# The first stage of a convolution and feed-forward kernel: other queue orders, integers cast by their transfers, x1 evicted in pairs, normalisation on POOL

## The reference

```
xn   = layernorm(x)                         # over the 256 features
# branch 1
z    = layernorm(xn) * gamma + beta
proj = z @ W_in + b_in                      # 768 columns: v, x1, x2 of 256 each
y    = causal_conv(v,  k0) * x1             # along the 4096 tokens, per channel
y    = causal_conv(y,  k1) * x2
a    = xn + y @ W_out + b_out
# branch 2
h    = silu(xn @ (w_gate/127).T) * (xn @ (w_up/127).T)
f    = h @ (w_down/127).T
out  = x + a + f
```

## Time and profile before

| what | value |
|---|---|
| median of three runs | 362.04 us |
| the profiled execution: its own time, its span | 361.94 us, 360.2 us |
| PE busy | 310.2 us, 86% |
| DVE busy | 250.2 us, 69% |
| POOL busy | 196.3 us, 54% |
| ACT busy | 182.8 us, 51% |
| mean granted TensorE clock | 0.957 |
| DMA | 81.00 MB, 225 GB/s on the mean |
| first matmul of the first convolution | 98.46 us from the span's start |

### The profile page before, as it was taken

The page is one execution under the profiler, slowest core; times in us unless marked ns, Lnnn a source line. Parts: engine busy times, 40 slices in busy tenths (PEclk is TensorE's granted clock), DMA queues, the critical chain, the costliest instruction groups (busy, mean ns, idle before and its releaser), DMA issues.

```text
span 360.2 us, 11764 instructions
## 1 busy us (share of the span) xinstructions
PE 310.2 (86%) x4940; PEld 243.2 (68%) x4940; DVE 250.2 (69%) x523; ACT 182.8 (51%) x383; POOL 196.3 (54%) x268
## 2 busy tenths in 40 slices
PE   0737573988398999999999999999999999998995
PEld 0425452777385777777777777877777776657994
DVE  1794996678436566666766668857766766787995
ACT  1464444799134444434444444444444444449993
POOL 3699077357746667567667675686676663210000
PEclk9976958799989999999999999999999999999999
DMA  7995300006068696786886887957868879500445
GB/s 252 341 340 163 131 1 2 4 12 224 2 235 322 226 387 243 278 349 237 322 326 249 352 291 262 379 226 300 348 230 332 323 251 378 206 0 3 140 154 177
DMA packets 22072, 81.00 MB, mean 225 GB/s; under 512 B 2050, under 2 KB 13186, under 8 KB 13826
## 3 DMA queue, kind: packets, MB, share of 16 engines
q1 hardware_dynamic: 21026, 79.04, 59.2%
q10 hardware_dynamic: 992, 1.18, 1.0%
HBM read 75.50 MB, written 4.72 MB: 223 GB/s over the span
## 4 chain that ended last, share of the span: by engine, by line
PE 55%; DVE 15%; ACT 11%; POOL 8%; issue 6%; DMA 3%; POOLq 0%; DVEq 0%; SPq 0%; ACTq 0%
PE bank_c L271 14%; PE bank_p L271 11%; PE bank_u L271 10%; PE bank_g L271 10%; PE bank_d L271 9%; ACT vx L695 3%; DMA res<-in_L_attn_x 3%; ACT vx L687 3%; DVE stats L726 2%; ACT xr L586 2%; DVE hhl L869 2%; DVE x1y L747 1%; DVE sgh L864 1%; DVE pmw L850 1%; ACT ybuf L575 1%
## 5 line engine op out<-in xcount | busy, mean ns | idle before, releaser
L271 PE MATMUL bank_d<-wd,hhl 128*128 128x256 f16 x384 | 84.3, 271 | 0.3 <-DVE hhl L869 0.2
L271 PEld LDWEIGHTS bank_p<-wq,xT 128*128 128x128 f16 x1536 | 71.5, 99 | 16.8 <-issue 1.7
L271 PE MATMUL bank_p<-wq,xT 128*128 128x64 f16 x1536 | 80.9, 194 | 2.1 <-issue 2.1
L271 PE MATMUL bank_u<-xT,wgu 128*128 128x512 f16 x192 | 66.2, 378 | 0.4 <-DVE sgh L864 0.4
L271 PE MATMUL bank_g<-xT,wgu 128*128 128x512 f16 x192 | 66.2, 377 | 0.0
L271 PEld LDWEIGHTS bank_c<-vhl,bands 128*128 128x128 f16 x1024 | 50.0, 97 | 22.5 <-issue 7.2
L271 PE MATMUL bank_c<-vhl,bands 128*128 128x64 f16 (+3 forms) x1024 | 58.3, 186 | 6.5 <-POOL vhl L1073 5.5
L271 PEld LDWEIGHTS bank_c<-ybuf,bands 128*128 128x128 f16 x1024 | 51.7, 96 | 17.9 <-issue 1.2
L1067 POOL TENSOR_TENSOR vx<-vx,bias 128x512 f32<-128x512 f32 x32 | 39.2, 1226 | 42.7 <-DVE vx L755 42.7
L271 PE MATMUL bank_c<-ybuf,bands 128*128 128x64 f16 (+3 forms) x1024 | 60.3, 184 | 0.8 <-DVE ybuf L889 0.8
L625 ACT CAST hhl<-sgh 128x512 f16<-128x512 f32 x48 | 29.7, 619 | 41.6 <-DVE sgh L864 41.6
(11 more groups left out here) (168 smaller groups left out, 539.7 us busy)
## 6 DMA issues: line engine op xcount, KB each, us to landing
bands<-taps_seq SPq DMA_DIRECT2D x64, 1024.0 KB, 8.1
out<-res SPq DMA_DIRECT2D x8, 512.0 KB, 2.9
res<-in_L_attn_x SPq DMA_DIRECT2D x3, 1024.0 KB, 10.4
res<-in_L_attn_x SPq DMA_DIRECT2D x2, 512.0 KB, 8.5
bands<-in_L_attn_W_in ACTq DMA_DIRECT2D x1, 768.0 KB, 5.9
bands<-in_L_ffn_w_gate SPq DMA_DIRECT2D x1, 768.0 KB, 10.0
bands<-in_L_ffn_w_up SPq DMA_DIRECT2D x1, 768.0 KB, 10.2
vx<-in_L_ffn_w_down SPq DMA_DIRECT2D x1, 768.0 KB, 10.1
```

The lines of the kernel that those rows point to most:

```text
L271: return nc.tensor.matmul(o, w, m, start=start, stop=stop, skip_group_check=True)
```

## The change

- SP's queue loads x blocks 0 to 3, then W_in, x 4 to 7, x 8 to 15, the taps, x 16 to 23, x 24 to 31, b_out, W_out. ACT's queue loads gamma and beta as two rows of 128 each (PE transposes them, a new step at the front of its program) and b_in. CUTS becomes 0, 4, 8, 16, 24, 32.
- POOL's queue loads the three integer tensors into float32 tiles, so the transfers cast them. `pair` on POOL is gone: PE transposes the unscaled values (`transpose_pair`), ACT rounds with the scale, DVE splits with the scale.
- ACT normalises blocks 0 to 7, POOL 8 to 31 (NA = 8).
- `project` trails the transposes by LV = 5 blocks, `project_x1` by LX = 8. x1 is evicted two blocks at a time and without its bias: pairs 0 to 9 by ACT (JA = 10), two instructions each, 10 to 15 by DVE, one instruction each. POOL adds the x1 bias a group of channels at a time, in the main stage one group ahead.
- The integer pairs come one a block from block 28 (PAIR0); the program branches after block 22 (FORK).
- DVE's statistics come one or two blocks at a time, its maxima at b = 10, 12 and 14, and the constants in four parts. POOL's taps and scales are spread over its loop.
- One residual ahead of the groups, not four; three in groups 1 to 3 and two in groups 4 to 14.

```diff
-    CUTS = (0, 4, 12, 20, 28, NB)
+    CUTS = (0, 4, 8, 16, 24, NB)
+    LV = 5
+    LX = 8
+    NA = 8
+    JA = 10
+    PAIR0 = 28
+    FORK = 22
...
+            load_x(0)
+            sp.dma_start(win[:, :, :], W_in.rearrange("(k p) n -> p k n", p=P)).then_inc(win_loaded, 16)
+            load_x(1)
+            load_x(2)
...
+            load_x(3)
+            load_x(4)
...
-                            sp.wait_ge(unit_ready, HB)
+                            sp.wait_ge(unit_tp, HB)
...
+            pe.wait_ge(gb_loaded, 32)
+            nc.tensor.transpose(w_bank[:, 0:2 * KD], gb_row[:, :], ident32[0:2 * KD, 0:2 * KD]).then_inc(gb_tp, 1)
...
-                pe.wait_ge(unit_ready, q + 1)
                 if q > 0:
                     pe.wait_ge(unit_l, q)
+                src, _ = pair_src(q)
...
+                if 0 <= b - LX < NB:
+                    project_x1(b - LX)
+                if 0 <= b - PAIR0 < PAIRS:
+                    transpose_pair(b - PAIR0)
...
+            def evict_x1(j):                                     # ACT
+                act.wait_ge(x1_mm, 2 * j + 2)
+                for b in (2 * j, 2 * j + 1):
...
+                    last = nc.scalar.activation(x1y2[:, :, b:b + 1].rearrange("p c o -> p (c o)"), o, ACT.Copy, scale=col(r2r, b))
+                last.then_inc(x1a_ready, 1)
...
+            def evict_x1(j):                                     # DVE
+                dve.wait_ge(x1_mm, 2 * j + 2)
...
+                nc.vector.tensor_tensor(x1y2[:, :, pair], bank_c[j % 2][:, :].rearrange("p (b c) -> p c b", b=2), scales,
+                                        ALU.mult).then_inc(x1v_ready, 1)
...
+            for b in range(1, NB + LX + 5):                      # DVE
+                if b <= 4:
+                    layernorm_stats(2 * b + 6, 2 * b + 8)
+                elif b <= 16:
+                    layernorm_stats(b + 11, b + 12)
+                elif b <= 18:
+                    layernorm_stats(2 * b - 6, 2 * b - 4)
                 if b - 1 < NB:
                     split_x(b - 1)
...
+                if b in (10, 12, 14):
+                    if b == 10:
+                        dve.wait_ge(int_loaded, 48)
...
+            def normalise(b):                                    # POOL
+                if b == NA or b in CUTS:
+                    pool.wait_ge(r_ready, batch_of(b) + 1)
+                pool.wait_ge(x_tp, b - 3)
+                nc.gpsimd.tensor_scalar(xn[:, b % 4, :], res[:, b, :], col(r1, b), col(nmr, b), ALU.mult, ALU.add).then_inc(xnp_ready, 1)
...
+            first_scales(0)
+            second_scales(0)
+            first_scales(1)
+
+            pool.dma_start(gu_f[:, 0:HB, :], w_gate.rearrange("(u p) d -> p u d", p=P)).then_inc(int_loaded, 16)
+            pool.dma_start(gu_f[:, HB:2 * HB, :], w_up.rearrange("(u p) d -> p u d", p=P)).then_inc(int_loaded, 16)
+            pool.dma_start(wd_f[:, :, :], w_down.rearrange("(a p) h -> p a h", p=P)).then_inc(int_loaded, 16)
+            second_scales(1)
+            for b in range(4, NB + LX):
+                if b == 4:
+                    first_scales(2)
+                if b == 5:
+                    second_scales(2)
+                if NA <= b + 2 < NB:
+                    normalise(b + 2)
+                if b == 7:
+                    pool.wait_ge(bin_ready, 1)
+                    nc.gpsimd.tensor_tensor(bias[:, :], bin_row, scl, ALU.mult).then_inc(bias_ready, 1)
+                if b in (8, 9):
+                    scale_taps(b - 8)
...
+                if b == 13:
+                    first_scales(3)
+                if b == 15:
+                    second_scales(3)
+                if b == 21:
+                    first_scales(4)
+                if b == 23:
+                    second_scales(4)
+                if b in (16, 24, 32, 38):
+                    add_bias((16, 24, 32, 38).index(b))
+                if b in (22, 30, 37):
+                    split_v((22, 30, 37).index(b))
+            split_v(3)
+            add_x1_bias(0)
...
             for G in range(NG):                                  # POOL
+                for b in residuals_of(G):
+                    residual(b)
                 gate_1(G, 0)
                 gate_1(G, 1)
+                if G < NG - 1:
+                    add_x1_bias(G + 1)
```

More of the change, by code:

```diff
@@ L479, in body @@
             def body(general):
-                for b in range(FORK, NB + 4):
+                for b in range(FORK, NB + LX):
                     first_stage(b)
@@ L554, in _ @@
             for dst, src, s in (
-                (win[:, :, :], W_in.rearrange("(k p) n -> p k n", p=P), win_loaded),
-                *((gb[:, i, k:k + 1], a[k * P:(k + 1) * P].rearrange("(p o) -> p o", o=1), gb_loaded)
-                  for i, a in enumerate((gamma, beta)) for k in range(KD)),
+                *((gb_row[i * KD:(i + 1) * KD, :], a.rearrange("(k p) -> k p", p=P), gb_loaded) for i, a in enumerate((gamma, beta))),
                 (bin_row[:, :], bass.AP(b_in.tensor, b_in.offset, [[0, P], [1, 3 * D]]), bin_loaded),
@@ L574, in normalise @@
                     act.wait_ge(x_tp, b - 3)
-                nc.scalar.activation(xn[:, b % 4, :], res[:, b, :], ACT.Identity, bias=col(nmr, b), scale=col(r1, b)).then_inc(xn_ready, 1)
+                nc.scalar.activation(xn[:, b % 4, :], res[:, b, :], ACT.Identity, bias=col(nmr, b), scale=col(r1, b)).then_inc(xna_ready, 1)
             def round_x(b):
@@ L1092, in taps, with split_taps, add_x1_bias @@
                 link(last)
-                for v, (taps, where) in enumerate(spans):
-                    nc.gpsimd.tensor_tensor(kpd[:, :, v, 1, where], taps, kpd[:, :, v, 0, where], ALU.subtract).then_inc(kpad_ready, 1)
+            def split_taps(v):
+                taps, where = spans[v]
+                nc.gpsimd.tensor_tensor(kpd[:, :, v, 1, where], taps, kpd[:, :, v, 0, where], ALU.subtract).then_inc(kpad_ready, 1)
+            def add_x1_bias(G):
+                if G == 0:
+                    pool.wait_ge(x1a_ready, JA)
+                    pool.wait_ge(x1v_ready, NB // 2 - JA)
+                tile = x1y2[:, G * CG:(G + 1) * CG, :]
+                row = bias[:, :]
+                off = bass.AP(row.tensor, row.offset + D + G * CG, [row.ap[0], [1, CG], [0, NB]])
+                nc.gpsimd.tensor_tensor(tile, tile, off, ALU.add).then_inc(x1_biased, 1)
@@ L1103, in _ @@
-            layernorm_scales(1)
-            taps()
-            layernorm_scales(2)
-            pool.wait_ge(bin_ready, 1)
-            nc.gpsimd.tensor_tensor(bias[:, :], bin_row, scl, ALU.mult).then_inc(bias_ready, 1)
-            layernorm_scales(3)
-            add_bias(0)
-            layernorm_scales(4)
-            pool.wait_ge(ffn_consts, 1)
-            for q in range(PAIRS):
-                if q == 3 or q == 7:
-                    add_bias((q + 1) // 4)
-                pair(q)
-                if q in (1, 5):
-                    split_v(q // 4)
@@ L1119, in _, with residuals_of @@
+            split_v(3)
+            add_x1_bias(0)
             pool.wait_ge(bout_loaded, 16)
             residual(0)
-            residual(1)
-            add_bias(3)
-            residual(2)
-            residual(3)
-            split_v(3)
+            def residuals_of(G):
+                first, n = (3 * G - 2, 3) if G < 4 else (2 * G + 2, 2)
+                return range(first, first + n) if 0 < G < NG - 1 else ()
             def gate_1(G, h):
```

276 lines of the change are left out of this document (150 added, 126 removed).

## The result

Four runs of the changed kernel took 350.55 to 354.43 us, median **352.55**. The kernel before took 362.05 beside them (360.8 to 362.51). The ratio is 0.9723, 95% interval 0.9686 to 0.976: faster by 2.8%. Forecast were 348.7 and a range of 343 to 358, so the time lies inside, 3.9 us above the forecast.

The account below looks back on a forecast made before the run. The middle was taken as bound by PE's own work, the first stage by several bounds in turn. S 13.6 us earlier and 0.4 more behind it give -13.2: 361.9 becomes 348.7 us, range 343 to 358.

Parts of the forecast that it names:

- S: Start of the first convolution, the one moment the change moves: 98.46 us before, forecast at 84.9.
- Step 1: Startup up to the scaled weights: ready at 14.8 us, against 20.17 before; the 5.4 us head start not all kept.
- Step 2: POOL until block 8: three transfers hold it 6.3 us at no cost; it normalises block 8 from 28.0 us.
- Step 3: Blocks 8 to 27: POOL becomes slowest; PE reaches the branch at about 52 us, gap 3.7, block 28 at 64.
- Step 4: Integer pairs, one a block from block 28, each waiting for the last: 2.03 us apiece, pair 8 starting at 81.4.
- Step 5: Behind S: POOL's x1 bias additions fall in its idle time; 0.4 us more, in group 0.
- A: First stage: integers land late, holding up DVE and then PE; 366 us, chance 0.08.
- B: Main stage: POOL's extra work surfaces, 0.37 to 0.6 us in each of 15 groups; 356 us, chance 0.13.
- C: First stage: POOL is a quarter slower than its quiet durations, 8 us on 34; 355 us, chance 0.14.
- D: First stage: branch gap partly hidden or ACT's eviction cheap, 3 to 5 us less; 344.5 us, chance 0.08.
- E: First stage hardly moves, the new order being held back elsewhere; time within 0.5%, chance 0.03.

Follow-up runs that it names:

- experiment 2: Changed kernel with the old queue order for W_in, gamma and beta, without PE's transpose of gamma and beta: 355.95 us.
- experiment 11: Changed kernel with ACT normalising all blocks again, and DVE's statistics in bursts with the three maxima together: 357.14 us.
- experiment 10: Changed kernel with all sixteen pairs of x1 blocks evicted by DVE, none by ACT (JA = 0): 352.79 us.
- experiment 5: Changed kernel with the integer pairs in two PSUM banks in turn, starting at block 31 instead of 28: 345.92 us.
- experiment 3: Changed kernel with an integer pair every second block from block 22 instead of one a block from 28: 345.5 us.
- experiment 12: Changed kernel with two pair banks from block 31, ACT normalising 12 blocks, residuals 0 to 5 in the first stage, last round_v ahead of last round_pair: 340.56 us.
- experiment 7: Changed kernel with POOL's sixteen additions of the x1 bias each replaced by an operation on one element: 351.2 us.
- experiment 1: Changed kernel with all 32 blocks normalised by ACT again (NA = 32): 353.81 us.

## Why the prediction was right, and where it was off

**Which number decides.** Right: the gain is the move of S. From S to the end the two profiled executions differ by 0.6 us. The 11.3 us of S are made up of 5.4 less up to block 8 (t(8) was 35.05), 6.8 less from there to block 16, 7.0 less from there to block 28 (19.9 for 26.8), and 7.9 more from block 28 to S (24.1 for 16.3), where the pairs now stand. PE's clock has a part that no run isolates: in the kernel before it was 0.51 from 45 to 54 us and 0.50 from 62 to 66.

**Step 1, scaled weights.** Forecast 14.8, measured 16.14. The square started at 7.50 for 7.0. The larger part is an order that I read and didn't price: the statistics of blocks 4 to 7 stand on DVE ahead of the column scales and wait for x, which landed at 10.1, so the scales started at 11.97, though PE's four matmuls ended at 10.78. The queue orders alone are worth 2.7 us of S (experiment 2).

**Step 2, POOL to block 8.** The three transfers took 1.08, 0.83 and 0.71 us of POOL, 2.6 for the 6.3 taken: SP's 2.17 was the wrong end. It changed nothing, since DVE's statistics were the later side, at 23.5 for 22.3, and POOL normalised block 8 at 29.05 for 28.0. By the Trainium skill ("DMA: Bandwidth & Descriptors", the anatomy of one DMA) such a transfer takes an estimated 3.8 us; here, with three of them and loads of x under way together, they landed 7.3 to 9.9 us after their issue, so that figure doesn't hold for such a crowd, and the measurement decides.

**Step 3, blocks 8 to 27.** POOL as the slowest engine: right up to the branch, with 0.562 us for a normalisation. PE reached the branch at 52.1 (52 forecast), the gap was 2.76 for 3.7, block 28 came at 63.07 for 64. But why the stage was faster is not what I credited. PE's time for blocks 8 to 16 fell from 20.3 to 13.5 us, 6.8, and that isn't due to POOL as normaliser alone (worth 0.6 of S) nor to the spread statistics alone (0.6): each covers for the other, and to lose both costs 4.0 of S, 3.4 of it in blocks 8 to 16 (experiment 11). DVE's burst and POOL's own lateness lie beside each other, so the later of the two is paid, not their sum. Which of the earlier scales, the smaller x1 evictions and the later projections brings the rest of the 6.8 us I haven't isolated; it isn't the engine that evicts, for t(16) is the same in experiment 10 (43.10). This stays open, and so does how the 7.0 us from block 16 to 28 divide.

**Step 4, the integer pairs: the term that was mis-sized.** Forecast 17.4 us from block 28 to pair 8, the ninth and last, measured 20.5. Three parts:
- seven rounds took 2.22 us for 2.03, 7 x 0.19 = 1.3: ACT's instruction, which now scales too, takes 0.69 for 0.58, DVE's 0.75 for 0.69. I had taken both from rows in which POOL had done the scaling;
- from pair 0 to pair 1 it was 3.4 us, 1.4 more than a forecast round: the first rounding stood on ACT behind `round_x`, `reverse_x` and an eviction of x1, and began at 66.45, though PE had started on pair 0 at 64.60. Without ACT's evictions this round takes 2.22 as well (experiment 10);
- 0.4 is before pair 0.

The end of the chain was better sized: from pair 8's start to S 3.6 us for 3.5. I named that only the ring paces the pairs, and didn't draw the consequence, that a second bank and a start at block 31 take away 6.4 us (experiment 5); spread over blocks the pairs cost little (experiment 3).

**Step 5, behind S.** Right in size, 0.6 for 0.4. In the first groups PE waits 0.89 and 1.81 us for DVE's L954, which is late behind POOL's and ACT's work on the same values. The timeline of the changed kernel:

```profile
91.67 0.86 DVE L954 SCALAR_TENSOR_TENSOR ybuf<-ybuf 128x512 f16<-128x512 f32 x1 [1.72 <-ACT ybuf L678]
92.78 0.26 PE L282 MATMUL bank_c<-ybuf,bands 128*128 128x64 f16 x4 [0.89 <-DVE ybuf L954]
...
105.30 1.05 POOL L1179 TENSOR_TENSOR x1y<-x1y,bias 128x512 f32<-128x512 f32 x1
...
107.15 0.26 PE L282 MATMUL bank_c<-ybuf,bands 128*128 128x64 f16 x4 [1.81 <-DVE ybuf L954]
```

The kernel before had a gap of 1.65 us of its own near the second place, so little of it is new. The first wait is 0.67 in experiments 5 and 12 alike, so the residuals aren't its cause; the second falls from 1.76 to 0.71 between these two, when the residuals leave group 1.

**Rivals.** A (late integers) is dead: the three overlapped and landed by 28 us. B (POOL surfaces in the main stage) is refuted by experiment 7: 1.3 us behind S for 5 or more, though the conflict itself is there. C (POOL slower beside DVE in the first stage): 0.562 us for 0.555, no. D: the branch gap was 0.9 smaller, but the 3 to 5 us of it went the other way in step 4. E: the pairs at the end did cost more than forecast, at their forecast place. The profiled execution lay 1.2 us below the median of its own kernel, where the forecast had it 0.1 below. Three later executions, of experiments 1, 3 and 10, show an additional PE gap "for issue" of 0.8 to 0.9 us in the main stage; what causes it stays open.

## What to carry to other kernels

Find the one moment that the change can move, and price the chain into it in program order on each engine: a rounding that stood behind other work on its own queue was nearly half of what the pairs took too long here. A sequence whose steps go through three engines and one buffer is paced by the round trip, whatever each engine's load, and a stretch of the profile in which no engine is full is where to look for it: a second buffer with its later start was worth more than half of the whole change. Two edits can cover for each other, so that undoing either alone shows nothing; undo both before you call them worthless. And a result of nothing can be two effects that cancel: compare the moments inside the stage, and take the spread of a moment from two executions whose programs are the same up to it.

## What was not expected of the hardware

- A casting transfer of 768 KB held POOL 0.71 to 1.08 us. Transfers of that size without a cast held SP's queue 2.17 us in the kernel before, at the end of a long list, and 0.49 us as the second of the changed kernel (W_in, at 1.22), so the cast isn't shown to cost anything and the place in the queue matters more.
- PE's gap at the branch was 3.70, 2.76 and 4.23 us ahead of blocks 17, 22 and 30; what it cost depended on whether PE was the late engine there.
- Behind the same gap of 2.8 to 3.1 us PE's granted clock fell from 1.00 to 0.50 in the changed kernel and in experiments 3 and 5, and stayed at 1.00 in experiment 7. It was worth about 1 us.
- ACT's eviction of 512 elements out of PSUM takes 0.69 us as an activation with a column scale, 0.58 as a cast.
- DVE's L954, which reads two operands from SBUF, takes 0.68 us alone, mostly 0.86 and up to 1.38 beside POOL's addition of the x1 bias; that addition takes 1.51 and 1.58 us instead of 1.05 in the two groups of the longest ones. This bears out the rule of the Trainium skill that the prediction names ("SBUF — State Buffer", on engine ports). It was cheap, because it is seldom on PE's path: at the two waits of step 5, leaving out the additions gave PE back 0.4 and 0.2 us.
